# Router logits taken from rows before their normalisation, and two projections moved two units later

## The reference

```python
p = einsum('blhd,dm->blhm', x, proj_mat) / sqrt(8)        # for q and for k
feat = concatenate([cos(p), sin(p)]) / sqrt(128)
kv = einsum('blhm,blhd->bhmd', feat_k, v); out = einsum('blhm,bhmd->blhd', feat_q, kv) @ Wo.T + bo
x = layernorm(x + out)
logits = einsum('bsd,de->bse', x, Wr) + br                # on the normalised rows
route_w = softmax(logits); best two, renormalised
x = layernorm(x + sum over the two of gate * (relu(x W1 + b1) W2 + b2))
```

## Time and profile before

| | |
|---|---|
| median of 3 runs | 565.49 us |
| the profiled execution | 564.61 us |
| its span, first to last instruction | 562.8 us |
| busy: PE, DVE, ACT, POOL | 480.8, 426.0, 409.5, 421.8 us |
| mean granted clock of TensorE | 0.936 of full |

### The profile page before, as it was taken

One profiled execution on the slowest core, in us unless ns is written; L12 is line 12 of the kernel. 1 busy time (PEld: TensorE's weight loads), 2 busy tenths in 40 slices (PEclk: granted clock), 3 DMA queues, 4 the chain that ended last, 5 costly groups with the idle time before them and its releaser, 6 DMA issues.

```text
span 562.8 us, 12567 instructions
## 1 busy us (share of the span) xinstructions
PE 480.8 (85%) x4206; PEld 304.8 (54%) x4206; DVE 426.0 (76%) x880; ACT 409.5 (73%) x538; POOL 421.8 (75%) x464
## 2 busy tenths in 40 slices
PE   4499889999999999999999899686999999999300
PEld 2343344444444444444444343566999999999300
DVE  5578988988989989989989978243777776777362
ACT  2297689798898898898797887304877777688044
POOL 2079969899899899899899868472777777777343
PEclk9699999999999999999999999955999999999755
DMA  6685304506405406316116232422222222221471
GB/s 70 177 228 162 105 1 142 132 11 174 104 29 140 120 29 156 100 41 182 43 57 159 55 114 82 145 76 63 68 72 73 69 69 77 68 77 40 132 264 75
DMA packets 43928, 56.02 MB, mean 100 GB/s; under 512 B 8807, under 2 KB 30937, under 8 KB 43865
## 3 DMA queue, kind: packets, MB, share of 16 engines
q1 hardware_dynamic: 38993, 45.84, 30.5%
...
...
## 4 chain that ended last, share of the span: by engine, by line
POOL 47%; PE 29%; issue 8%; DMA 5%; DVE 5%; ACT 4%; SPq 0%; ACTq 0%; DVEq 0%; POOLq 0%
POOL feats L1209 16%; POOL routed_dram L1277 13%; PE ang L687 10%; PE misc L696 10%; POOL parts L304 4%; POOL qk_f L302 3%; POOL parts L306 3%; POOL hot L1256 2%; PE misc L507 1%; POOL rstd L1217 1%; PE ang L678 1%; ACT feats L854 1%; PE ang L487 1%; POOL slot_k L1269 1%; DMA out<-feats 1%
## 5 line engine op out<-in xcount | busy, mean ns | idle before, releaser
L925 DVE TENSOR_SCALAR turns<-ang 128x1024 f16<-128x1024 f32 x128 | 155.3, 1216 | 36.5 <-PE ang L478 24.8
L747 ACT ACTIVATE feats<-ang 128x1024 f32<-128x1024 f32 x128 | 131.7, 1029 | 58.6 <-PE ang L487 56.5
L1209 POOL TENSOR_TENSOR feats<-feats 128x1024 f32<-128x1024 f32 x56 | 110.5, 1982 | 38.0 <-ACT feats L748 37.9
L748 ACT ACTIVATE feats<-ang 128x1024 f32<-128x1024 f32 x128 | 131.5, 1028 | 0.0
L816 ACT ACTIVATE feats<-weights_mem 128x1156 f32 x72 | 83.7, 1164 | 32.8 <-DVE feats L1156 28.4
L933 DVE TENSOR_TENSOR feats<-feats 128x1024 f32<-128x1024 f32 x72 | 106.8, 1484 | 0.7 <-ACT feats L748 0.6
L1277 POOL DMA_INDIRECT routed_dram<-rows_s,slots x64 | 83.4, 1303 | 18.8 <-issue 18.3
L1305 POOL DMA_INDIRECT expert_dram<-feats x72 | 70.7, 982 | 24.9 <-DVE feats L1156 15.4
L487 PE MATMUL ang<-turns,negi 128*128 128x512 f16 x256 | 77.5, 384 | 5.6 <-DVE turns L925 4.9
L687 PE MATMUL ang<-feats 128*128 128x128 f32 x576 | 78.2, 280 | 2.0 <-DVE feats L1111 2.0
L696 PE MATMUL misc<-feats 128*128 128x128 f32 x576 | 77.0, 278 | 0.0
...
## 6 DMA issues: line engine op xcount, KB each, us to landing
...
```

Source lines behind the costliest of these rows:

```text
L747: act.activation(f[:, 0, :], a, ACT.Sin, scale=TWO_PI)
L748: act.activation(f[:, 1, :], a, ACT.Sin, scale=TWO_PI / 2).then_inc(s["sines"], 1)
L925: dve.tensor_scalar(turns[:, u % 2, :], ang[:, slot(ph, u), :], MAGIC, -MAGIC, ALU.add, ALU.add)\
L1209: pool.tensor_tensor(f, f, f, ALU.mult).then_inc(s["sq_p"], 1)
```

## The change

Three things change together.

1. The logits come from `y`, the rows before their normalisation. A normalised row is y * rstd + shift, with one rstd and one shift per row, so its logits are rstd * (y Wr) + shift * (column sums of Wr) + br. `rows_T` transposes `y` and waits for `y_ok` instead of `xn_ok`. `take_logits` becomes four DVE instructions (one per 128 rows) that multiply by `rstd` and add `corr`. `corr` = shift * `wr_sums` + br is two further POOL instructions at the end of `rsqrt`, one waiting for the other. `wr_sums` is made once, in batch 0, by one PE product (unit 11) and one ACT instruction (unit 12).
2. The order within a batch: `rows_T` and `logits` go from units 8 and 9 to 6 and 7, `project` of k and q from 6 and 7 to 8 and 9, with their companions: `rows_evac` from 8 to 6, `proj_evac` from 6 and 7 to 8 and 9, `normalize` from 7 to 9, `take_logits` and the best two from 10 to 8, `chosen` from 11 to 9, the two splits on POOL from 7 and 9 to 10 and 11.
3. After the last batch `rows_T` and `logits` stand ahead of the first half of `expert_biases` instead of behind it, on ACT `rows_evac` ahead of the copies of the biases.

```diff
--- before.py
+++ after.py
@@ -169,6 +169,8 @@
         mv = sb("mv", [P, LT, 2])
         rstd = sb("rstd", [P, LT])
         shift = sb("shift", [P, LT])
+        wr_sums = sb("wr_sums", [P, EXP])
+        corr = sb("corr", [P, LT, EXP])
         fflat = feats[:, :, :, :].rearrange("p a b c -> p (a b c)")
         experts = weights_mem[:, :].rearrange("p (e n) -> p e n", e=EXP)
@@ -554,21 +556,25 @@
                                    start=True, stop=True)
                 mm.then_inc(s["wo_mm"], 1)
-            def rows_T(b, *free):
-                wait(pe, "xn_ok", 1, b, 1)
-                wait(pe, *free)
-                for t in range(LT):
-                    mm = pe.transpose(misc[:, 1, t * P:(t + 1) * P], rows_s[:, t, 0:P], ident[:, :])
+            def rows_T(b):
+                wait(pe, "y_ok", 1, b, 1)
+                for t in range(LT):
+                    mm = pe.transpose(misc[:, 1, t * P:(t + 1) * P], y[:, t, :], ident[:, :])
                 mm.then_inc(s["xr_mm"], 1)
-            def logits(b, *free):
+            def logits(b):
                 wait(pe, "xr_ev", 1, b, 1)
-                wait(pe, *free)
                 for t in range(LT):
                     mm = pe.matmul(misc[:, 1, t * EXP:(t + 1) * EXP], xr_T[:, t * P:(t + 1) * P], wr_s[:, :],
                                    start=True, stop=True)
                 mm.then_inc(s["lg_mm"], 1)
+            def column_sums():
+                pe.wait_ge(s["wload"], 16 * N_WLOADS)
+                pe.wait_ge(s["q_ev"], 2)
+                pe.matmul(misc[:, 1, 0:EXP], minus_2[:, :], wr_s[:, :], start=True, stop=True).then_inc(s["sum_mm"], 1)
             def ranks(b, *free):
@@ -609,20 +615,22 @@
                         kv_product(b, KV_STEP.index(u), *(("v_ev", 1, b, 1) if last else ("xT_ev", 1, b, 2)))
                     if u == 4 and not first:
                         wo_product(b - 1)
-                    if u == 6 and not last:
-                        project(0, 1, b + 1, *(("v_ev", 1, b, 1) if first else ("y_ok", 1, b, 0)))
-                    if u == 7 and not last:
+                    if u == 6 and not first:
+                        rows_T(b - 1)
+                    if u == 7 and not first:
+                        logits(b - 1)
+                    if u == 8 and not last:
+                        project(0, 1, b + 1, *(("v_ev", 1, b, 1) if first else ("lg_ok", 1, b, 0)))
+                    if u == 9 and not last:
                         project(1, 1, b + 1, "k_ev", 1, b, 2)
-                    if u == 8 and not first:
-                        rows_T(b - 1, *(("y_ok", 1, b, 0) if last else ("q_ev", 1, b, 2)))
-                    if u == 9 and not first:
-                        logits(b - 1, "xr_ev", 1, b, 0)
+                    if first and u == 11:
+                        column_sums()
                     if u == 12:
                         kv_turn(b)
                         if not first:
-                            ranks(b - 1, "lg_ok", 1, b, 0)
+                            ranks(b - 1, *(("lg_ok", 1, b, 0) if last else ("q_ev", 1, b, 2)))
                     if u == 13:
-                        out_product(b, 0, 0, *(("q_ev", 1, b, 2) if first else ("based", 1, b, 0)))
+                        out_product(b, 0, 0, *(("sum_ok", 1, b, 1) if first else ("based", 1, b, 0)))
                         out_product(b, 0, 1)
                     if u == 14:
                         c_product(b)
@@ -663,9 +671,9 @@
                                        start=False, stop=(j == HT - 1))
                 mm.then_inc(s["b2_mm"], 1)
+            rows_T(e - 1)
+            logits(e - 1)
             expert_biases(0, EXP // 2)
-            rows_T(e - 1, "y_ok", 1, e, 0)
-            logits(e - 1, "xr_ev", 1, e, 0)
             ranks(e - 1, "lg_ok", 1, e, 0)
             expert_biases(EXP // 2, EXP)
@@ -778,11 +786,14 @@
                 for u in range(UNITS):
                     if u == 3 and not first:
                         out_evac(b - 1)
-                    if u == 7 and not first:
+                    if first and u == 12:
+                        act.wait_ge(s["sum_mm"], 1)
+                        act.activation(wr_sums[:, :], misc[:, 1, 0:EXP], ACT.Copy, scale=-0.5).then_inc(s["sum_ok"], 1)
+                    if u == 9 and not first:
                         normalize(b - 1)
-                    if u in (6, 7) and not last:
-                        proj_evac(b + 1, u - 6, 1)
-                    if u == 8 and not first:
+                    if u in (8, 9) and not last:
+                        proj_evac(b + 1, u - 8, 1)
+                    if u == 6 and not first:
                         rows_evac(b - 1)
                     sines(b, ph, u)
@@ -790,6 +801,7 @@
             out_evac(BATCH - 1)
+            rows_evac(BATCH - 1)
             act.wait_ge(s["b1_mm"], 1)
             b1_T = banks[5][:, 0:EXP * HT]
             act.activation(experts[:, :, AT_B1:WROW], b1_T.rearrange("p (e j) -> p e j", e=EXP), ACT.Copy,
@@ -797,7 +809,6 @@
             act.activation(b1_s[:, :], b1_T, ACT.Copy).then_inc(s["b1_ok"], 1)
             normalize(BATCH - 1)
-            rows_evac(BATCH - 1)
             act.activation(warm[:, :], zero_t[:, :], ACT.Sigmoid)
             for h in range(2):
                 act.wait_ge(s["b2_mm"], h + 1)
@@ -975,8 +986,12 @@
             def take_logits(b):
                 wait(dve, "lg_mm", 1, b, 1)
-                dve.tensor_tensor(lg[:, :, :], misc[:, 1, 0:LT * EXP].rearrange("p (t e) -> p t e", e=EXP),
-                                  over(br_bc[:, :].unsqueeze(1), tile8), ALU.add).then_inc(s["lg_ok"], 1)
+                wait(dve, "corr_ok", 1, b, 1)
+                for t in range(LT):
+                    ins = dve.scalar_tensor_tensor(out=lg[:, t, :], in0=misc[:, 1, t * EXP:(t + 1) * EXP],
+                                                   scalar=rstd[:, t:t + 1], in1=corr[:, t, :],
+                                                   op0=ALU.mult, op1=ALU.add)
+                ins.then_inc(s["lg_ok"], 1)
             def largest(b):
                 hold(dve, "lg_ok", 1, b, 1)
@@ -1023,9 +1038,9 @@
             dve.wait_ge(s["raw_T"], 3)
             dve.tensor_copy(woT[:, :], misc[:, 0, 0:P]).then_inc(s["raw_ev"], 1)
-            BEFORE_ROUND = ((6, moments), (10, take_logits), (13, move_base))
-            AFTER_ROUND = ((5, residual), (10, largest))
-            AFTER_SQUARE = ((5, statistics), (10, which), (12, take_ranks), (13, slot_numbers))
+            BEFORE_ROUND = ((6, moments), (8, take_logits), (13, move_base))
+            AFTER_ROUND = ((5, residual), (8, largest))
+            AFTER_SQUARE = ((5, statistics), (8, which), (12, take_ranks), (13, slot_numbers))
             def body(b, ph):
                 first = isinstance(b, int) and b == 0
@@ -1217,6 +1232,13 @@
                 pool.tensor_tensor(rstd[:, :], rstd[:, :], half_t[:, :], ALU.pow).then_inc(s["ln_pow"], 1)
                 wait(pool, "ln_pow", per, n, base + 1)
                 pool.tensor_tensor(shift[:, :], shift[:, :], rstd[:, :], ALU.mult).then_inc(s["ln_shift"], 1)
+                wait(pool, "ln_shift", per, n, base + 1)
+                pool.wait_ge(s["sum_ok"], 1)
+                pool.tensor_tensor(corr[:, :, :], over(shift[:, :].unsqueeze(2), tile8),
+                                   over(wr_sums[:, :].unsqueeze(1), tile8), ALU.mult).then_inc(s["corr_1"], 1)
+                wait(pool, "corr_1", per, n, base + 1)
+                pool.tensor_tensor(corr[:, :, :], corr[:, :, :], over(br_bc[:, :].unsqueeze(1), tile8), ALU.add)\
+                    .then_inc(s["corr_ok"], 1)
             def body(b, ph):
@@ -1234,10 +1256,10 @@
                         pool.tensor_tensor(xb, xb, bo_bc[:, :, :], ALU.add).then_inc(s["bo_ok"], 1)
                     if u == 6 and not first:
                         rsqrt(1, b - 1, 0)
-                    if u in (7, 9) and not last:
-                        split(pool, b + 1, (u - 7) // 2)
-                    if u == 11 and not first:
+                    if u == 9 and not first:
                         chosen(b - 1)
+                    if u in (10, 11) and not last:
+                        split(pool, b + 1, u - 10)
                     if u == 13 and not first:
                         slots_of_picks(b - 1)
                     if u in (14, 15) and not first:
@@ -1254,6 +1276,7 @@
                 ins.then_inc(s["off_ok"], 1)
                 hold(pool, "off_ok", 1, b, 1)
                 pool.tensor_scalar(hot[:, :, :, :], hot[:, :, :, :], 0.0, None, ALU.is_equal).then_inc(s["hot_ok"], 1)
+                hold(pool, "scattered", 16 * TOPK * LT, b, 0)
                 wait(pool, "hot_ok", 1, b, 1)
                 pool.tensor_tensor(picks[:, :], hot[:, 0, :, :].rearrange("p t e -> p (t e)"),
                                    hot[:, 1, :, :].rearrange("p t e -> p (t e)"), ALU.add).then_inc(s["picked"], 1)
@@ -1273,6 +1296,7 @@
```

(1 more changed line is left out.)

2 lines of the change are left out of this document (1 added, 1 removed).

## The result

The changed kernel takes 596.17 us (median of 4 runs, 594.82 to 597.65); the kernel before took 565.83 in the same session. The ratio is 1.0529, interval 1.0489 to 1.0569. Forecast were 572.4, and 581 as the upper end. The sign was right and the size was not. Executions of one kernel can differ by several per cent: the ratios leave the disturbed ones out, while medians and profiles may include them.

The account below looks back on a forecast made before the run. POOL's work was taken to bound the kernel, its 41.04 us being the period. Terms of +8.3 (six periods), +1.0 (batch 0), -0.4 (last body) and -2.0 (tail) sum to +6.9: 572.4 us against 565.5, range 559 to 581 with rivals.

Parts of the forecast that it names:

- POOL's work is the period in the old order: One period of the kernel before: POOL never waits, so its work, 41.04 us, is the period.
- 12.6 us from K to the sines of unit 8: Within a batch, new order: 10.66 us to the end of unit 8's subtraction, then sines of about 1.95.
- K: Start of PE's key product in unit 5, which waits for POOL's square of unit 1; the cycle is counted from it.
- the two new waits on POOL: POOL idle 1.5 us before the choice, for DVE's best two, and 0.4 to 1.4 us for the sines of unit 8.
- The chain behind it: POOL runs without idling from the sines of unit 8 to the next batch's unit 1 square; period 42.6 us, not 41.04.
- The second path: DVE's slot reduction waits for POOL; PE comes 2.1 us later, less 1.06 won, and 1.1 later at unit 12: also 42.6.
- The k parts: Split 10 us later, through DRAM by K + 24.6, needed at K + 28: hidden by 3 us.
- The port rival: Splits and five DVE squares collide on the SBUF port: 44 us per period, 580.9 us in total; chance 12%.
- The rule against the row: A DVE square with two SBUF inputs delays a scatter by about 1 us, though the Trainium skill infers the opposite.
- The correction: Two dependent POOL instructions add 0.64 us per period; DVE's wait for corr costs nothing unless corr meets a square.
- The last body: The 0.79 us wait for normalised rows goes and 0.4 comes back at unit 12: -0.4 us.
- The tail: After the last batch, ranks at 364.3 behind four biases taking 5.9 us, first scatter at 366.0: -2.0 us.

Follow-up runs that it names:

- 8: Kernel before, with the correction for the last batch only and the ranks behind three expert biases, one ahead of the transposes: 559.56 us, ratio 0.9925.
- 11: Kernel before, with DVE's reduction to slot numbers behind the square of unit 14 instead of 13: 563.87 us, ratio 1.0002.
- experiment 7: Changed kernel, after the last batch one expert bias ahead of the transposes, two behind the logits, then ranks, then the other five: 587.64 us, ratio 1.0396.
- 6: Changed kernel, with DVE's reduction to slot numbers behind the square of unit 14 instead of 13: 590.89 us, ratio 1.0517.
- 10: Changed kernel, with query parts moved only after the scatters, slot reduction behind unit 14's square, and ranks behind three expert biases: 583.73 us, ratio 1.0297.
- 9: Changed kernel, with four scatters sent behind unit 14 and the other four after the square at unit 3 of the next batch: 588.02 us, ratio 1.0440.
- 12: Changed kernel, with an added POOL multiplication of 256 elements per partition behind each of the four first-choice scatters, batches 0 to 6: 601.23 us, ratio 1.0686.
- 5: Changed kernel, from batch 2 on each read of key and query parts brings only the first sixteenth of its columns: 578.42 us, ratio 1.0253.

## Why the prediction was wrong

- **POOL's work is the period in the old order.** True of the profile that it was read from, and not of the old order in general: in four of the six periods of 8 and 11 POOL has some 2.2 us less to do, stands 1.7 us for sines, and the period is still 41.0. What sets it there was not looked into.
- **12.6 us from K to the sines of unit 8.** Right. In the batch that escaped (experiment 7) K is 121.18, the sines of unit 8 end at 133.82, 12.6 us behind it, and the square of unit 8 starts at 134.09. Of the two new waits on POOL one is there, 1.03 us before the choice; the choice then takes 2.8 us with a port wait, and POOL doesn't stand for the sines of unit 8.
- **The chain behind it.** Two splits 7.0 (forecast 7.82), square of unit 10 2.9 (1.85), slots 0.4 (1.40), square of unit 12 1.9 (1.85), scatters with the hole before them 12.6 (13.1), square of unit 1 1.9 (1.9). K to K is 121.18 to 163.40, 42.2 us, against 42.6. That the sum fits so well is in part luck, since errors of up to 1.1 us cancel. Its last link is loose too: the square of unit 1 ends at 162.72, 0.7 us before K, and PE doesn't wait for it, so in this batch POOL's chain alone doesn't set K.
- **The second path.** In the changed kernel DVE waited 2.21 us for the slot products (2.1 forecast), PE 1.01 at unit 12 (1.1), and there is no wait before the transposes. Not priced: PE's wait of 1.19 at unit 15.
- **The k parts.** Right: the first of their four groups is read in by 238.75 and used at 243.40.
- **The step that failed** is the 42.6 as the sum of a chain: "scatters 13.1, square of unit 1 1.9", with the sines of unit 1 taken as ready. In five periods the scatters took 10.5 to 11.2 us, and POOL stood 3.4 to 3.5 us for sines behind them, because TensorE's signals came late: 44.0 to 47.5. The term was +8.3 for six periods and measured +26.5 (273.2 against 246.7, cut to cut). Of this the chain explains 6 x 1.4 = 8 us (an estimate, from the 42.3 to 42.7 of undisturbed batches); the other 18 are the late signals, for which the sum had no term. The port rival (580.9) had the right sign and another mechanism: the scatters became shorter, not longer. Among the variants its mechanism shows, in 6 and 10.
- **The rule against the row.** The square of DVE from 152.33 to 153.55 in the batch that escaped [experiment 7] stands beside the scatter from 152.48, which took 1.90 us; one without a square beside it took 0.96. The Trainium skill (SBUF — State Buffer, "Who interferes with whom") infers that such a square does not delay it. This trace disagrees again.
- **The correction.** 0.53 us on POOL, 0.64 forecast. That DVE's wait for it "costs nothing unless corr meets a square" was wrong: corr met none (0.24 and 0.25 us), and DVE waited 0.81 us in the batch at 218.22, 8.0 in all eight.
- **Batch 0:** +1.0, as forecast. **The last body:** +0.7 where -0.4 was forecast; where it was lost was not taken apart.
- **The tail: -2.0 forecast, +2.0 measured.** The picks came as said (5.9 us behind the cut, forecast 5.5). The failing term is that four biases "take what they took, 5.9". They did so before because they began while PE was still at full clock. PE in the changed kernel:

```profile
386.63 0.79 PE L666 MATMUL ang<-b_s,ident 8*128 8x128 f32 x2 [0.38 <-ACT b_s L809]
387.35 2.08 PE L669 MATMUL ang<-weights_mem,b_s 128*128 128x128 f32 x8
...
397.40 0.23 PE L585 MATMUL misc<-picks,tri 128*128 128x32 f16 x1
```

2.7 us a bias at a granted clock of 0.51, the 1.2 GHz level, make 10.8 instead of 5.9, and the ranks stand behind them at 397.40 though the picks were there at 390.68. Experiments 7 and 8 took this back.

**Open.** What holds the signals physically. The profile's end of a matmul is computed, and by the Trainium skill (Perfetto Trace Analysis, "Tensor Engine Instruction (MATMUL, LD_WEIGHTS)") the signal follows only once PSUM has acknowledged the writes and it has been propagated; the delays of 1 to 5 us agree with that order, and nothing in these traces looks inside it. The runs show that the delays go with the scatters (9), that they are gone where the scatters are spaced (12), that they are smaller with fewer bytes of reads (5), and that the same code can escape (7). Whether it is POOL's issuing or the scatters' traffic that holds them was not separated. Why the old order nearly always escapes is only argued. Its second and fifth scatter are stretched to 1.96 by DVE (13 us in all); a late DVE stretches them less, which may make the next signals later still. Experiment 7 fits such a feedback but shows no more than its first step.
